# A product made in four pieces, the second half of it behind the first half's sums

## The chip, the cores and the metric

The kernel runs on one core of a Trainium2 chip. The metric is the time of one execution of the whole program on the device, in microseconds (us). Below, TensorE is PE in the profile, VectorE is DVE, ScalarE is ACT, GpSimd is POOL and SyncE is SP; a trailing "q" is the engine's sequencer.

## The reference

A graph with 12,500 nodes of 64 features and 400,000 edges, sorted by destination, goes through two graph layers with a residual and a layer norm each. The change is in the message passing of the second layer:

```
h     = x @ Wn.T + bn                                   # 12,500 x 64
w     = ssp(ssp(edge @ We1.T + be1) @ We2.T + be2)      # 400,000 x 64, ssp(z) = softplus(z) - log 2
m     = h[src] * w                                      # 400,000 x 64
agg   = segment_sum(m, dst)                             # 12,500 x 64
x     = layernorm(x + (ssp(agg @ Wc.T + bc) @ Wp.T + bp))
```

## The kernel before

The program has three long phases over the edges: two for the first graph layer (`pick_phase`, called twice) and a third, `gate_phase`, for the lines above. Each goes over 125 blocks (`NB`) of 3,200 edges, as 128 partitions with 25 edges each (the slots, `SLOTS`).

In the third phase a block n needs these things.

- **Rows.** 22 of the 25 slots of `h[src]` are gathered from `hn_table` in memory by indirect DMAs that GpSimd issues, one for each slot (L965), into the buffer `big[:, u]` with u = n mod 2. GpSimd waits on `block_used` before it begins: TensorE counts that up when it has read the second half of the sums of block n-2 (L1022). So the gather for block n+2 begins when block n's second sums are done. SyncE loads the next list of indices (L939) as soon as a gather has landed. The last three slots (`GSEL`) are picked by TensorE products with one-hot matrices (`pick`, L1002, one call for each slot) and finished on VectorE (`take`: L1148, L1159, L1162).
- **Gates.** TensorE makes the first layer's product (`first_layer`, L983) two blocks ahead, ScalarE its softplus logs (`first_logs`, L1060 to L1064), VectorE its activation (`first_activation`, L1129), TensorE the second product (`second_layer`, L990), VectorE adds the bias (`second_values`, L1136), ScalarE takes the second logs (`second_logs`, L1058 to L1064, four groups of columns, written to `lg2`), and VectorE adds the two parts (`gates`, L1143). `gates` writes over the same tile that `second_logs` writes: `gate_e` is `lg2`. So `second_logs(n+1)` must not begin before block n's gates have been read.
- **Messages.** `gate_messages` (L1190 to L1196) waits for the gather and multiplies: `big = (gate_e - log 2) * big`, all 25 slots x 64 = 1600 elements a partition in one VectorE instruction. It then counts up `gated`. TensorE waits for `gated` in `add_up(0)`, and ScalarE waits for it at the head of `second_logs(n+1)` (L1078).
- **Sums.** The slots are in two halves, 0 to 12 and 13 to 24 (`HALVES`). For each half VectorE makes a one-hot tile (`make_hot`, L1170), TensorE multiplies the messages with it (`add_up(h)`, L1018), and VectorE adds the result into `acc` (L1188).

Each engine works through its own list in a fixed order, written by hand. For block n:

```
VectorE: gate_messages(n); half(0): hot, wait for TensorE, acc; take(n+1, 0); gates(n+1);
         window loads; half(1): hot, wait for TensorE, acc; take(n+1, 1);
         first_activation(n+2); take(n+1, 2); second_values(n+2); window loads of block n+1
TensorE: pick(n+1, 0); add_up(0); pick(n+1, 1); first_layer(n+2);
         add_up(1); pick(n+1, 2); second_layer(n+2)
ScalarE: second_logs(n+1); first_logs(n+2); low_hots(n+2)
GpSimd:  gather of block n+2 once add_up(1) of block n is done
```

A "window load" is a short run of VectorE sequencer work (`windows`) that reads the bounds of a loop from memory; the engine is idle if nothing is queued before it.

Of the kernel before, what the change touches and what calls it, by code (L numbers as in the profile page):

```python
# [17 lines left out]
ALU = mybir.AluOpType  # L18
# [6 lines left out]
F = 64  # L25
H = 16
LOG2 = 0.6931471805599453
EPS = 1e-5

SLOTS = 25  # L30
# [3 lines left out]
HALVES = ((0, 13), (13, SLOTS))  # L34
GROUPS = ((0, 4), (4, 7), (7, 10), (10, 13))
NG = len(GROUPS)

WIN = 128
NW = -(-V // WIN)
# [48 lines left out]
def gnn_kernel(nc, x, xw, src, src_sel, src_gate, dst_all, edge_t, W_linT, b_lin, W1_agg, W1_root, b1, W2_parts, W2_diag, WnT, bn, We1T, be1,  # L88
               We2T, be2, WcT, bc, WpT, bp, out):
    ctx = ExitStack()  # L90
    with ctx:
# [6 lines left out]
        def sem(name):  # L98
            return ctx.enter_context(nc.semaphore(name))
# [75 lines left out]
        big = sb("big", [P, 2, SLOTS * F])  # L175
# [35 lines left out]
        waited = sem("waited")  # L211
# [655 lines left out]
        def gate_phase(tag, table, buf, hots, tiles):  # L867
# [6 lines left out]
            s1, gate_e = lg1, lg2  # L874
# [23 lines left out]
            z2_psum = sem(f"{tag}_z2_psum")  # L898
            u_made = sem(f"{tag}_u_made")
            log2_made = sem(f"{tag}_log2_made")  # L900
            gated = sem(f"{tag}_gated")
            pZ = bank[2:6]

            def turn_of(g, u):
# [17 lines left out]
            with nc.Block() as block:  # L922
# [48 lines left out]
                @block.tensor  # L971
                def _(pe):
                    pe.sem_inc(block_used, bufs)
                    pe.sem_inc(hot_used[0], 1)
                    pe.sem_inc(hot_used[1], 1)

                    def first_layer(n, turn, u):
                        pe.wait_ge(e_in[u], 16 * turn)
                        for q in range(NG):
                            cs, w = cols_of(q)  # L980

                            pe.wait_ge(u_made, NG * n + q + 1)
                            pe.matmul(pZ[q][:, 0:w], we1_2[:, :], xT_e[u][:, cs], start=True,  # L983
                                      stop=True).then_inc(z1_psum, 1)

                    def second_layer(n):
                        for q, (a, b) in enumerate(GROUPS):
                            pe.wait_ge(s1_made, NG * n + q + 1)
                            for k in range(a, b):
                                last = pe.matmul(pZ[q][:, (k - a) * P:(k - a + 1) * P], s1[:, k * P:(k + 1) * P],  # L990
                                                 we2_2[:, :], start=True, stop=True)
                            last.then_inc(z2_psum, 1)

                    def pick(n, s):
                        pe.wait_ge(low_made, GSEL * n + s + 1)
                        for c in range(2):
                            half = 2 * s + c
                            o = bank[HALF_BANK[half % 3]][:, 0:GHALF * F]
                            pe.wait_ge(pick_taken, 2 * GSEL * n + half + 1)
                            for h in range(GLOW):  # L1000
                                for part in range(2):
                                    last = pe.matmul(o, low_hot[s][:, h, :],  # L1002
                                                     hn_split[:, part, h * GHIGH + c * GHALF:h * GHIGH + (c + 1) * GHALF, :],
                                                     start=(h == 0 and part == 0), stop=(h == GLOW - 1 and part == 1))
                            last.then_inc(pick_psum, 1)

                    def add_up(h, n, u):
                        a, b = HALVES[h]
                        since, to, _ = windows(pe, n, h, False)
                        if h == 0:  # L1010
                            pe.wait_ge(gated, n + 1)
                        pe.sem_inc(waited, 1)
                        with pe.Fori(since, to) as visit:
                            pe.wait_ge(acc_added[h], visit + 1)
                            pe.wait_ge(hot_made[h], visit + 1)
                            for j in range(a, b):
                                c = (j % 2) * F
                                last = pe.matmul(sums[h][c:c + F, :], buf[u][:, j, 0:F], hots[h][:, j - a, :],  # L1018
                                                 start=(j < a + 2), stop=(j >= b - 2))
                            last.then_inc(hot_used[h], 1)  # L1020
                        if h == 1:
                            pe.drain().then_inc(block_used, 1)  # L1022

                    def body(n, g, u):
                        more = not isinstance(n, int) or n + 2 < NB
                        pick(n + 1, 0)
                        add_up(0, n, u)
                        pick(n + 1, 1)
                        if more:
                            first_layer(n + 2, turn_of(g, u) + 1, u % 2)  # L1030
                        add_up(1, n, u)
                        pick(n + 1, 2)
                        if more:
                            second_layer(n + 2)

                    first_layer(0, 1, 0)
                    second_layer(0)
                    pick(0, 0)
                    first_layer(1, 1, 1)
                    pick(0, 1)  # L1040
                    pick(0, 2)
                    second_layer(1)
                    with pe.Fori(0, turns) as g:
                        for u in range(bufs):
                            body(bufs * g + u, g, u)
                    for n in range(bufs * turns, NB - 1):
                        body(n, n // bufs, n % bufs)
                    add_up(0, NB - 1, (NB - 1) % bufs)
                    add_up(1, NB - 1, (NB - 1) % bufs)

                @block.scalar
                def _(act):
# [19 lines left out]
                    def second_logs(n):  # L1072
                        for q in range(NG):
                            cs, w = cols_of(q)

                            act.wait_ge(u_made, NG * n + q + NG + 1)
                            if q == 0 and (not isinstance(n, int) or n > 0):
                                act.wait_ge(gated, n)  # L1078
                            log_of(lg2[:, cs], u_e[:, cs], None, log2_made)

                    def low_hots(n, s, turn, u):
# [34 lines left out]
                def _(dve):  # L1116
# [59 lines left out]
                    def half(h, n, since, to, first):  # L1176
                        with dve.Fori(since, to) as visit:
                            window = nc.s_assert_within(
                                visit - since, 0, NW - 1,
                                skip_runtime_bounds_check_because="a half's dst span NW windows at most")  # L1180
                            start = nc.s_assert_within(
                                first + window * WIN, 0, V - 1,
                                skip_runtime_bounds_check_because="a visit starts at or before a dst")
                            make_hot(h, n, window, visit + 1)

                            dve.wait_ge(hot_used[h], visit + 2)
                            a_w = acc[:, bass.ds(start, WIN)]
                            dve.tensor_tensor(a_w, a_w, sums[h], ALU.add).then_inc(acc_added[h], 1)  # L1188

                    def gate_messages(n, g, u):  # L1190
                        dve.wait_ge(gathered[u], 16 * took * (g + 1))
                        dve.sem_inc(waited, 1)
                        dve.drain()
                        h = big[:, u, :]
                        dve.scalar_tensor_tensor(h, gate_e[:, 0:SLOTS * F], -LOG2, h, ALU.add,  # L1195
                                                 ALU.mult).then_inc(gated, 1)  # L1196

                    def body(n, g, u):
                        ahead = not isinstance(n, int) or n + 1 < NB
                        more = not isinstance(n, int) or n + 2 < NB  # L1200
                        since, to, first = windows(dve, n, 0, True)
                        gate_messages(n, g, u)
                        half(0, n, since, to, first)
                        if ahead:
                            take(n + 1, 0, (u + 1) % 2)
                            gates(n + 1)
                        since, to, first = windows(dve, n, 1, True)
                        half(1, n, since, to, first)
                        if ahead:
                            take(n + 1, 1, (u + 1) % 2)  # L1210
                        if more:
                            first_activation(n + 2)
                        if ahead:
                            take(n + 1, 2, (u + 1) % 2)
                        if more:
                            second_values(n + 2)
# [535 lines left out]
```

## Time and profile before

| | |
|---|---|
| median of 3 runs | 14133.36 us (14097.36 to 14136.13) |
| the profiled execution | 14125.89 us, its span 14124.2 us |
| TensorE busy | 9348.3 us, 66% |
| ScalarE busy | 6242.7 us, 44% |
| GpSimd busy | 6000.3 us, 42% |
| VectorE busy | 5042.0 us, 36% |
| mean granted TensorE clock | 0.782 of full speed |

No engine is busy for more than two thirds of the span, and the DMA engines only for a tenth or so. The first `gate_messages` of the third phase begins at 7614.7 us and the last of its 125 at 14049.6 us. In the rows below a time is the start of an instruction in us from the start of the span, then comes its length in us; x26 means that 26 such instructions ran with no gap; what stands in brackets is the idle time of the engine just before and what ended it. A TensorE row can be off in its names, since some of its records can be missing.

### The profile page before, as it was taken

How to read it: one execution, taken by the hardware profiler on the slowest of the kernel's cores; microseconds unless marked ns; L12 is line 12 of the kernel's file. 1: busy time of each engine (PE TensorE's matmuls, PEld its weight loads, DVE VectorE, ACT ScalarE, POOL GpSimd, SP SyncE). 2: the span in 40 equal slices, each digit the busy share in tenths (PEclk: the TensorE clock that was granted, in tenths of full speed). 3: DMA queues.
4: the chain of work that ended last, by engine and by line, in shares of the span. 5: the costliest groups of instructions: out<-in, count | busy, mean ns of one | idle time of the engine just before them, and what ended most of it. 6: DMA issues, size and time to landing. Idle time of an engine off the chain costs nothing. (4 is left out here: it accounts for less than half of the span.)

```text
span 14124.2 us, 173836 instructions
## 1 busy us (share of the span) xinstructions
PE 9348.3 (66%) x50412; PEld 8170.3 (58%) x50413; DVE 5042.0 (36%) x7217; ACT 6242.7 (44%) x11176; POOL 6000.3 (42%) x6363
## 2 busy tenths in 40 slices
PE   5666666666676666766676666666666666666666
PEld 5666666666666666666665554455445544555444
DVE  3333333333333333333334333333333333333334
ACT  3444444444344444444444444444444444444444
POOL 4444444444344444444433334433443334433343
PEclk8888888888788888888887777777777777777777
DMA  1111111111111111111111111111111111111111
GB/s 50 22 21 21 21 21 22 21 21 21 25 21 21 21 21 22 21 21 21 21 25 50 33 32 31 33 33 32 31 33 33 32 31 33 33 33 32 31 33 37
DMA packets 337142, 392.85 MB, mean 28 GB/s; under 512 B 163119, under 2 KB 238563, under 8 KB 336564
## 3 DMA queue, kind: packets, MB, share of 16 engines
q0 software_dynamic: 200000, 147.86, 7.2%
q1 hardware_dynamic: 136750, 244.13, 5.3%
q8 instruction: 34, 0.56, 0.0%
q14 instruction: 36, 0.29, 0.0%
q10 hardware_dynamic: 322, 0.03, 0.0%
HBM read 375.60 MB, written 15.95 MB: 28 GB/s over the span
## 5 line engine op out<-in xcount | busy, mean ns | idle before, releaser
L733 PE MATMUL banks<-split_sb,e_low_hot 128*128 128x400 f32 x22000 | 4648.8, 373 | 424.9 <-issue 357.3
L733 PEld LDWEIGHTS banks<-split_sb,e_low_hot 128*128 128x128 f32 x22000 | 4437.8, 209 | 556.9 <-issue 472.5
L965 POOL DMA_INDIRECT big<-hn_table,src_i x2750 | 2594.9, 944 | 3898.3 <-PEq L1022 3083.2
L1002 PE MATMUL banks<-hn_split,e_low_hot 128*128 128x448 f32 x10500 | 2913.9, 415 | 1996.4 <-issue 1994.8
L1002 PEld LDWEIGHTS banks<-hn_split,e_low_hot 128*128 128x128 f32 x10500 | 2232.4, 217 | 2586.9 <-issue 2428.9
L704 ACT ACTIVATE e_low_hot<-e_key_off 128x1536 fp32r<-128x1536 f16 x1000 | 1379.4, 1379 | 3719.3 <-remote 2416.1
L679 POOL DMA_INDIRECT big<-h_table,src_i x1750 | 1652.6, 944 | 1933.4 <-DVEq L846 1403.9
L679 POOL DMA_INDIRECT big<-p_table,src_i x1750 | 1652.8, 944 | 1920.5 <-DVEq L846 1394.6
L794 DVE TENSOR_REDUCE picked<-banks 128x48 f32<-128x1200 f32 x1000 | 1303.3, 1303 | 2851.9 <-remote 1834.2
L700 ACT ACTIVATE e_key_off<-e_key_in,node_off 128x384 f16<-128x384 f16 (+1 forms) x4000 | 2027.0, 577 | 127.6 <-DMA e_key_in<-sel_dram 43.7
L751 PE MATMUL banks<-hot,big 128*64 128x128 bf16 x6250 | 385.3, 259 | 1868.3 <-issue 985.6
L1058 ACT ACTIVATE e_wide<-e_wide 128x512 f32<-128x512 f32 x500 | 268.9, 538 | 2954.8 <-DVE big L1195 2922.2
L751 PEld LDWEIGHTS banks<-hot,big 128*64 128x64 bf16 x6250 | 265.4, 129 | 2024.9 <-issue 2024.6
L1136 DVE TENSOR_TENSOR e_wide<-banks,be_wide 128x512 f32<-128x512 f32 x500 | 276.2, 586 | 2555.0 <-remote 2257.6
L1089 ACT ACTIVATE e_low_hot<-spare,node_off 128x128 fp32r<-128x128 f16 x2625 | 802.5, 386 | 11.1 <-remote 11.1
L1018 PE MATMUL banks<-hot,big 128*64 128x128 f32 x6250 | 560.2, 341 | 371.9 <-DVE hot L1170 371.9
L1018 PEld LDWEIGHTS banks<-hot,big 128*64 128x64 f32 x6250 | 490.7, 175 | 500.3 <-issue 500.3
L835 DVE TENSOR_TENSOR acc<-acc,banks 128x128 f32 x500 | 144.2, 288 | 1516.9 <-PE banks L751 1073.3
L1159 DVE TENSOR_TENSOR spare<-banks,spare 128x448 f32<-128x448 f32 x750 | 445.1, 622 | 433.1 <-remote 322.0
L1060 ACT ACTIVATE e_wide<-banks,c_be 128x512 f32<-128x512 f32 x500 | 297.2, 594 | 649.4 <-PE banks L983 649.4
L1064 ACT ACTIVATE e_wide<-e_wide 128x512 f32<-128x512 f32 x1000 | 550.7, 551 | 68.0
L1062 ACT ACTIVATE e_wide<-e_wide 128x512 f32<-128x512 f32 x1000 | 550.7, 551 | 67.9
(221 smaller groups left out, 5237.0 us busy)
## 6 DMA issues: line engine op xcount, KB each, us to landing
e_wide<-in_edge_t SPq DMA_DIRECT2D x125, 832.0 KB
e_key_in<-sel_dram SPq DMA_DIRECT2D x250, 343.8 KB
big<-hn_table,src_i POOLq DMA_INDIRECT x2750
big<-p_table,src_i POOLq DMA_INDIRECT x1750
big<-h_table,src_i POOLq DMA_INDIRECT x1750
spare<-gate_dram SPq DMA_DIRECT2D x125, 96.0 KB
src_i<-in_src SPq DMA_DIRECT2D x375, 12.5 KB, 2.5
e_key_in<-sel_dram SPq DMA_DIRECT2D x250, 8.2 KB
```

The costliest lines, as they stand in the source:

```text
L679: pool.indirect_dma_start(buf[u][:, j, 0:ROW0], None, table, bass.IndirectOffsetOnAxis(ap=src_i[u][:, j:j + 1], axis=0),).then_inc(gathere ...
L700: act.activation(off[:, h, :], key_in[u][:, es], ACT.Abs, bias=node_off[:, h:h + 1])
L704: act.activation(low_hot[gr][:, :, :], off, ACT.Relu, bias=1.0, scale=-1.0).then_inc(low_made, 1)
L733: last = pe.matmul(o, low_hot[gr][:, h, e], split_sb[:, part, h * HI1:(h + 1) * HI1, :], start=(h == 0 and part == 0), stop=(h == HI2 - 1 ...
L751: last = pe.matmul(sums[h][c:c + ROW0, :], buf[u][:, j, :], hots[h][:, j - a, :], start=(j < a + 2), stop=(j >= b - 2))
L794: dve.tensor_reduce(picked[:, AT[gr]:AT[gr] + SIZE[gr], :], found, AX.X, ALU.max).then_inc(pick_taken, 1)
L965: pool.indirect_dma_start(buf[u][:, j, 0:F], None, table, bass.IndirectOffsetOnAxis(ap=src_i[u][:, j:j + 1], axis=0),).then_inc(gathered[u ...
L1002: last = pe.matmul(o, low_hot[s][:, h, :], hn_split[:, part, h * GHIGH + c * GHALF:h * GHIGH + (c + 1) * GHALF, :], start=(h == 0 and part ...
L1018: last = pe.matmul(sums[h][c:c + F, :], buf[u][:, j, 0:F], hots[h][:, j - a, :], start=(j < a + 2), stop=(j >= b - 2))
L1062: act.activation(o, o, ACT.Exp, scale=-1.0)
L1064: act.activation(o, o, ACT.Ln, bias=1.0).then_inc(made, 1)
L1089: act.activation(hot[:, h, :], key_in[u][:, s * P:(s + 1) * P], ACT.Abs, bias=node_off[:, h:h + 1])
```

## The change

The product of gates and rows is made in four instructions in place of one: slots 0 to 5 and 6 to 12 at the place where the one stood, and slots 13 to 18 and 19 to 24 after the first half's sums are in `acc` and before `take(n+1, 0)`. There are now two counters, one for each half. TensorE waits for the first in `add_up(0)` and for the second in `add_up(1)`. ScalarE, which waited for the one counter at the head of `second_logs(n+1)`, now waits for that of the second half.

```diff
+GATE_CUT = (((0, 6), (6, 13)), ((13, 19), (19, SLOTS)))
...
-            gated = sem(f"{tag}_gated")
+            gated = [sem(f"{tag}_gated{h}") for h in range(2)]
...
                     def add_up(h, n, u):
                         a, b = HALVES[h]
                         since, to, _ = windows(pe, n, h, False)
-                        if h == 0:
-                            pe.wait_ge(gated, n + 1)
+                        pe.wait_ge(gated[h], n + 1)
                         pe.sem_inc(waited, 1)
...
                             act.wait_ge(u_made, NG * n + q + NG + 1)
                             if q == 0 and (not isinstance(n, int) or n > 0):
-                                act.wait_ge(gated, n)
+                                act.wait_ge(gated[1], n)
                             log_of(lg2[:, cs], u_e[:, cs], None, log2_made)
...
-                    def gate_messages(n, g, u):
-                        dve.wait_ge(gathered[u], 16 * took * (g + 1))
-                        dve.sem_inc(waited, 1)
-                        dve.drain()
-                        h = big[:, u, :]
-                        dve.scalar_tensor_tensor(h, gate_e[:, 0:SLOTS * F], -LOG2, h, ALU.add,
-                                                 ALU.mult).then_inc(gated, 1)
+                    def gate_messages(h, n, g, u):
+                        if h == 0:
+                            dve.wait_ge(gathered[u], 16 * took * (g + 1))
+                            dve.sem_inc(waited, 1)
+                            dve.drain()
+                        for a, b in GATE_CUT[h]:
+                            m = big[:, u, a * F:b * F]
+                            last = dve.scalar_tensor_tensor(m, gate_e[:, a * F:b * F], -LOG2, m, ALU.add, ALU.mult)
+                        last.then_inc(gated[h], 1)
...
                         since, to, first = windows(dve, n, 0, True)
-                        gate_messages(n, g, u)
+                        gate_messages(0, n, g, u)
                         half(0, n, since, to, first)
+                        gate_messages(1, n, g, u)
                         if ahead:
                             take(n + 1, 0, (u + 1) % 2)
                             gates(n + 1)
```

## Rows read from the trace of the kernel before

**Rows 1.** Page: busy time of each engine, share of the span, instructions.

```profile
PE 9348.3 (66%) x50412; PEld 8170.3 (58%) x50413; DVE 5042.0 (36%) x7217; ACT 6242.7 (44%) x11176; POOL 6000.3 (42%) x6363
```

**Rows 2.** One line of the source, L1195, the product, over the whole span.

```profile
L1195 DVE SCALAR_TENSOR_TENSOR big<-e_wide,big x125: 1824/1825/1827, 7614.7 to 14049.6; 128x1600 f32<-128x1600 f32 x125
```

**Rows 3.** Timeline of all engines, block A, to its gather's landing.

```profile
10070.31 1.49 DVE L1136 TENSOR_TENSOR e_wide<-banks,be_wide 128x384 f32<-128x384 f32 x3 [5.65 <-remote]
10072.79 1.82 DVE L1195 SCALAR_TENSOR_TENSOR big<-e_wide,big 128x1600 f32<-128x1600 f32 x1 [0.99 <-issue]
10074.53 1.94 DVE L1170 SCALAR_TENSOR_TENSOR hot<-dst_f,win_base,banks 128x1664 f32<-128x1664 f32 x1
10074.71 0.63 ACT L1058 ACTIVATE e_wide<-e_wide 128x512 f32<-128x512 f32 x1 [23.07 <-DVE big L1195]
...
10076.62 3.07 PE L1018 MATMUL banks<-hot,big 128*64 128x128 f32 x26 [1.71 <-DVE hot L1170]
...
10079.91 0.29 DVE L1188 TENSOR_TENSOR acc<-acc,banks 128x128 f32 x1 [3.44 <-PE banks L1018]
...
10081.00 0.53 ACT L1064 ACTIVATE e_wide<-e_wide 128x384 f32<-128x384 f32 x1
...
10082.82 2.09 DVE L1143 SCALAR_TENSOR_TENSOR e_wide<-e_wide 128x512 f32<-128x512 f32 x4
10084.82 1.80 DVE L1170 SCALAR_TENSOR_TENSOR hot<-dst_f,win_base,banks 128x1536 f32<-128x1536 f32 x1
...
10085.40 2.96 PE L983 MATMUL banks<-e_wide,we 128*128 128x512 f32 x8
...
10088.29 1.53 PE L1018 MATMUL banks<-hot,big 128*64 128x128 f32 x24
...
10090.69 0.94 POOL L965 DMA_INDIRECT big<-hn_table,src_i  x1 [24.40 <-PEq L1022]
...
10119.51 0.33 SPq L939 DMA_DIRECT2D src_i<-in_src  x1
```

**Rows 4.** Timeline of all engines, block B, the next one.

```profile
10124.81 1.82 DVE L1195 SCALAR_TENSOR_TENSOR big<-e_wide,big 128x1600 f32<-128x1600 f32 x1 [1.50 <-issue]
...
10128.64 1.71 PE L1018 MATMUL banks<-hot,big 128*64 128x128 f32 x26 [1.87 <-DVE hot L1170]
...
10130.58 0.29 DVE L1188 TENSOR_TENSOR acc<-acc,banks 128x128 f32 x1 [2.08 <-PE banks L1018]
...
10133.03 0.53 ACT L1064 ACTIVATE e_wide<-e_wide 128x384 f32<-128x384 f32 x1
...
10136.29 1.81 DVE L1170 SCALAR_TENSOR_TENSOR hot<-dst_f,win_base,banks 128x1536 f32<-128x1536 f32 x1 [0.70 <-issue]
...
10138.95 1.53 PE L1018 MATMUL banks<-hot,big 128*64 128x128 f32 x24
...
10141.40 0.94 POOL L965 DMA_INDIRECT big<-hn_table,src_i  x1 [23.57 <-PEq L1022]
...
10175.07 1.82 DVE L1195 SCALAR_TENSOR_TENSOR big<-e_wide,big 128x1600 f32<-128x1600 f32 x1 [1.76 <-issue]
```

**Rows 5.** Timeline of all engines, block C, one with late second sums.

```profile
10905.98 1.82 DVE L1195 SCALAR_TENSOR_TENSOR big<-e_wide,big 128x1600 f32<-128x1600 f32 x1 [0.98 <-issue]
...
10913.25 0.29 DVE L1188 TENSOR_TENSOR acc<-acc,banks 128x128 f32 x1 [3.59 <-PE banks L1018]
...
10922.94 1.53 PE L1018 MATMUL banks<-hot,big 128*64 128x128 f32 x24
...
10925.34 0.94 POOL L965 DMA_INDIRECT big<-hn_table,src_i  x1 [25.82 <-PEq L1022]
...
10959.50 1.82 DVE L1195 SCALAR_TENSOR_TENSOR big<-e_wide,big 128x1600 f32<-128x1600 f32 x1 [1.90 <-issue]
```

**Rows 6.** Windows: us, busy us (instructions) of five engines, PEclk, DMA, GB/s.

```profile
10076.00:10079.00 3.00, 2.38 (x23) 2.41 (x25) 0.47 (x1) 2.73 (x7) 0.00 (x0) 0.50 0.00 0
10088.00:10090.00 2.00, 1.82 (x26) 1.29 (x24) 0.00 (x0) 1.86 (x4) 0.00 (x0) 1.00 0.35 57
```

## The prediction

> **What bounds the kernel now.** I read the page first. No engine is busy for more than two thirds of the span, and VectorE, which does the changed work, for 36% [rows 1]. So the kernel is held by an order of waits, and a saved microsecond counts only where it stands on that order. The view of the one source line gives the frame: 125 products of 1.82 us each, the first at 7614.7 us and the last at 14049.6 us [rows 2]. That is 6434.9 us over 124 steps, 51.9 us a block, and the change touches nothing outside this stretch.
>
> Then I read the timeline of three blocks and wrote every event as a distance from the start of the block's product. In block A [rows 3]: first one-hot tile 1.74, first sums on TensorE 3.83, first add into `acc` 7.12, `gates` 10.03, second one-hot tile 12.03 to 13.83, `first_layer` 12.61 to 15.57, second sums 15.50, first gather instruction 17.90, gather landed 46.72 (SyncE's next index load), next block's product 52.02. The reader is to see three things.
>
> First, from 17.90 on only the gather counts. It takes 28.8 us to land, and the product comes 5.3 us after the landing (10119.51 and 10124.81), just behind the last groups of `second_values` (the first row of block A, released 2.48 us before its product). From the gather's start to the next product it is 34.1 us in A, 33.7 in B and 34.2 in C, while the gather's start itself is at 17.9, 16.6 and 19.4 [rows 3 to 5]. The block lengths follow: 52.0, 50.3 and 53.5 us. A block is the gather's start plus about 34 us. I don't know why `second_values`, whose input comes from TensorE alone, waits that long; the release is shown as "remote". But the sum holds in three blocks whose gather starts 2.8 us apart, and both readings (the release waits for the gather, or for TensorE's own work behind the second sums) move with the second sums.
>
> Second, the second sums wait for TensorE, not for VectorE. In A the second one-hot tile is done at 13.83 and TensorE comes at 15.50, straight from `first_layer`. That is a slack of 1.7 us; it is 0.7 us less the usual handover in B, where the tile ends at 13.29 and TensorE comes at 14.14 [rows 4].
>
> Third, ScalarE stood idle for 23.07 us and begins `second_logs` 1.92 after the product's start, on the product's own signal. Its four groups take until 8.74, that is 6.82 us, and lie under the first one-hot tile, the first sums and `take` [rows 3].
>
> **The change part by part.** *Shorter first product.* In block A 1600 elements cost 1.74 us from start to next start, and four instructions with 1664 elements together 2.09 us to their end [rows 3]; the one long one needs 1.82 to its end, so the last end adds 0.08. The two equations (1600 c + k = 1.74 and 1664 c + 4 k = 2.01) give c = 1.045 ns an element and k = 0.07 us an instruction. Slots 0 to 5 are 384 elements, 0.47 us; slots 6 to 12 are 448, 0.54 us. The first one-hot tile starts at 1.00 in place of 1.74: 0.74 us saved. TensorE waited 1.71 us for that tile in A and 1.87 in B, so it takes all of it. If instructions did not overlap at all I would add 0.08 for each, and save 0.66; that is the lower bound.
>
> The Trainium skill, VectorE: DVE Perf Modes, The DRAIN you can't avoid, says that a next operation does not start until the pipeline has emptied. The trace differs: the one-hot tile starts 1.74 us after a product that lasts 1.82 [rows 3]. By the page the saving would be the 0.66 us just bounded.
>
> *Second product.* It starts where `take` started, 0.29 us after the first add, and its two pieces of 384 elements need 0.47 and 0.55: the second signal comes 1.31 us after the start of the add. In A that is 7.12 - 0.74 + 1.31 = 7.69.
>
> *The moved wait of ScalarE.* This is the term that decides. `second_logs(n+1)` may not write the gates' tile before the second product has read it, so it begins 0.10 us after that signal (1.92 against 1.82 before), at 7.79 and no longer at 1.92. After 6.82 us the last group is ready, at 14.61. What lies behind the wait on ScalarE, `first_logs` and `low_hots`, starts a little later too: its first input is ready about when `first_layer` starts, 12.61 - 0.74, and it now waits until 14.61. Its results are needed by `second_layer` and the next `pick`, behind the second sums, which move further than that; I price it at nothing. SyncE's two waits on these have tens of microseconds in hand.
>
> *VectorE behind it.* `take(n+1, 0)` is cover of some 2.7 us only; then `gates` waits group by group for ScalarE. Behind the last of those waits stand the window loads and the second one-hot tile. Block B shows this chain when ScalarE is the last: its last log ends at 10133.56 and the second tile starts at 10136.29, 2.73 us later, with VectorE idle for 0.70 of it [rows 4]. So in A the tile starts at 14.61 + 2.73 = 17.34, ends 1.81 later, and TensorE, by the 0.15 us from tile end to first sums in A, starts the second sums at 19.30. Before it was 15.50: 3.80 us later. `pick(n+1, 2)`, `second_layer` and the drain that lets the gather go are queued behind them.
>
> *By block.* New start = old first add + 12.18 us. A: 19.30, B: 17.95, C: 19.45, against 15.50, 14.14 and 16.96 [rows 3 to 5]. The second sums are 3.8, 3.8 and 2.5 us later, on average 3.4. C is less since TensorE was late there anyway.
>
> *The clock.* TensorE now has nothing to do from 15.57 - 0.74 = 14.83 to 19.30, 4.5 us in each block. In A the clock was at 0.50 (1.2 GHz) in the first sums, behind a wait of 1.71 us, and at 1.00 in the second ones [rows 6]; 26 matmuls took 3.07 us there, while in B they took 1.71 after a wait of 1.87 us. So after a wait the clock may be at either level. The second sums, 24 matmuls, would take 3.07 x 24 / 26 = 2.83 us at the lower one in place of 1.53: 1.3 us more, at most. The first sums could gain as much in blocks where their shorter wait keeps the clock up. I take 0.4 net, three blocks in ten, between the ends 0 and 1.3.
>
> *Sum.* 3.4 + 0.4 = 3.8 us a block for the 123 blocks that start a gather: 467 us. The profiled execution took 14125.9 us (span 14124.2), which gives 14593; it is 7 us under the median of the runs, inside their spread of 39 us. I predict 14590 us, 3.2% more.
>
> **The rivals.** *The low clock in every block.* For it: an idle stretch of 4.5 us, longer than the 1.71 before the slow first sums of A. Against it: B, fast after 1.87. Price: (3.4 + 1.3) x 123 = 578 us, 14704 us. The Trainium skill, TensorE: Matmul & The Clock Gate, What's actually happening, has the default clock throttled and activity releasing it; by that rule the second sums behind the new wait would be the slow ones, and rows 6 agree for the first sums of A.
>
> *Partly given back.* The time from the gather's start to the product shrinks when the start is late, say because part of what VectorE and ScalarE do behind it was late for its own reasons. A third to two thirds of 3.4 us, 14270 to 14410 us. Against it: 34.2 us in C, the block with the latest start.
>
> *Nothing is passed on.* The next product is set by something that does not move with the second sums. Then the 3.4 us vanish in the 34, and the time is 14126 us. The three block lengths speak against it.
>
> *Faster.* The first sums come 0.74 us sooner, and with them `pick`, `first_layer`, the second sums and the gather: 123 x 0.74 = 91 us, 14035 us. One thing decides: the second tile must be ready when TensorE arrives, at 15.50 - 0.74 = 14.76 in A. It needs 12.18 us from the old first add and may take 7.64. ScalarE's 6.82 us would have to be 2.3, or `second_logs` start before the second product, which its wait forbids.
>
> **How the numbers follow.** The forecast has 0.70, the low clock 0.12, partly given back 0.10, nothing passed on 0.04, faster 0.04. The forecast's own range comes from 2.9 to 4.7 us a block: all blocks like C with the clock term give 2.5 + 0.4, and the clock rival is the upper end: 14480 to 14704. With a little of the partial case below and a margin above, 14440 to 14730 us holds it 8 times in 10. A measurement of this kernel tells about 0.3%, 42 us, from no change: faster 0.04, same 0.04, slower 0.92.
>
> **What would show it.** In the new profile: two pairs of products in a block, near 1.0 us each pair; the first one-hot tile 1.00 us after the first piece; ScalarE's first log of `second_logs` 7.8 us after it (6.4 in blocks like B) and its idle time before grown; VectorE idle between the four `gates`, released by ScalarE; the second tile at 17.3, TensorE's second sums near 19.3 with the tile named as the releaser; the gather's start near 21.7, and 34 us from there to the next product. The clock row of the second sums tells the clock term. The prediction is wrong if those 34 us shrink, or if the second sums still follow `first_layer` without a wait.

## The result and the profile after

| | before | after |
|---|---|---|
| median of 4 runs each, side by side | 14115.88 us (14097.36 to 14136.13) | 14649.35 us (14623.76 to 14671.31) |
| ratio, 95% interval | | 1.0376 (1.0364 to 1.0388) |
| the profiled execution | 14125.89 us | 14671.31 us, its span 14669.6 us |
| mean granted TensorE clock | 0.782 | 0.772 |

The change makes the kernel 3.8% slower. The forecast was 14590 us, in the range 14440 to 14730 us; the measured time is 59 us above the forecast and inside the range. The two profiled executions differ by 545 us, 4.43 us for each of the 123 blocks, and the medians by 533 us, 4.34 us a block, where the forecast had 3.8.

In the comparisons below the kernel before takes about 14,120 us in some and about 8,320 us in others, once each way on the same chip, so every ratio is taken only against the runs of the kernel before that stood beside it, and each experiment says which of the two it met.

The page after, busy time of each engine; it answers to [rows 1]:

```profile
PE 9567.3 (65%) x50412; PEld 8315.3 (57%) x50413; DVE 5104.3 (35%) x7592; ACT 6240.6 (43%) x11176; POOL 6000.2 (41%) x6363
```

VectorE has 375 instructions more, three a block, and 62.3 us more work, 0.5 us a block. ScalarE and GpSimd have the same work as before. The 545 us are waits, and the slower clock in which TensorE's 219 us more are spent. The waits of the third phase after, from the view of waits (engine, line, what released it: us in total, times, longest):

```profile
ACT e_wide L1058 <- DVE big L1197: 3903.3, 124, 33.4
POOL big L966 <- PEq L1022: 3616.1, 123, 47.9
...
PE banks L1018 <- DVE hot L1170: 998.4, 248, 13.1
...
DVE e_wide L1143 <- ACT e_wide L1064: 326.1, 372, 1.0
DVE hot L1170 <- issue: 264.4, 124, 2.2
```

Before, the same view of the same phase had ScalarE at 2922.2 us behind the product, GpSimd at 3083.2 us behind TensorE, TensorE at 360.3 us in 125 waits behind the one-hot tile, no wait of `gates` for ScalarE at all, and 9.8 us idle before the second one-hot tile. The reader is to see the new chain in these five rows: ScalarE starts later (+981 us; in exchange its 642.7 us of waiting for TensorE's `first_layer`, 123 times, is gone), `gates` now waits for it (three times a block, since the first of the four logs is ready), the second tile stands behind the window loads (2.1 us a block; the row says "issue", and that it is the loads is read from the order of the code), TensorE waits for that tile as well as for the first (248 waits, not 125), and GpSimd waits 533 us more, 4.3 us a block.

The timeline after, one block, answers to [rows 3]; a time is the start, then come the length, and in brackets the idle time before and its releaser:

```profile
10104.17 1.09 DVE L1197 SCALAR_TENSOR_TENSOR big<-e_wide,big 128x384 f32<-128x384 f32 x2 [2.29 <-issue]
10105.18 1.94 DVE L1170 SCALAR_TENSOR_TENSOR hot<-dst_f,win_base,banks 128x1664 f32<-128x1664 f32 x1
...
10107.27 3.22 PE L1018 MATMUL banks<-hot,big 128*64 128x128 f32 x26 [10.34 <-DVE hot L1170]
...
10110.71 0.29 DVE L1188 TENSOR_TENSOR acc<-acc,banks 128x128 f32 x1 [3.59 <-PE banks L1018]
10110.92 1.02 DVE L1197 SCALAR_TENSOR_TENSOR big<-e_wide,big 128x384 f32<-128x384 f32 x2
...
10112.03 0.63 ACT L1058 ACTIVATE e_wide<-e_wide 128x512 f32<-128x512 f32 x1 [32.23 <-DVE big L1197]
...
10117.36 2.96 PE L984 MATMUL banks<-e_wide,we 128*128 128x512 f32 x8
...
10118.33 0.52 ACT L1064 ACTIVATE e_wide<-e_wide 128x384 f32<-128x384 f32 x1
...
10118.89 0.56 DVE L1143 SCALAR_TENSOR_TENSOR e_wide<-e_wide 128x384 f32<-128x384 f32 x1 [1.03 <-ACT e_wide L1064]
...
10121.59 1.81 DVE L1170 SCALAR_TENSOR_TENSOR hot<-dst_f,win_base,banks 128x1536 f32<-128x1536 f32 x1 [2.14 <-issue]
...
10123.55 2.83 PE L1018 MATMUL banks<-hot,big 128*64 128x128 f32 x24 [3.23 <-DVE hot L1170]
...
10127.29 0.94 POOL L966 DMA_INDIRECT big<-hn_table,src_i  x1 [29.80 <-PEq L1022]
```

Counted from the product's start: first tile 1.01, second product 6.75, ScalarE's first log 7.86 (before 1.92), its last log over at 14.68, the second tile 17.42 (before 12.03), second sums 19.38 (before 15.50), gather 23.12 (before 17.90). The next product came at 10160.84, 33.55 us after the gather's start. And the second sums take 2.83 us where they took 1.53 [rows 3]. The windows after show the clock in which they ran (us, busy us with counts of PE, PEld, DVE, ACT, POOL, then the granted clock, DMA share, GB/s); they are the first sums, `first_layer`, the two halves of the gap behind it, and the second sums:

```profile
10107.30:10110.50 3.20, 3.20 (x27) 2.87 (x27) 0.00 (x0) 0.00 (x0) 0.00 (x0) 0.50 0.00 0
10117.40:10120.30 2.90, 2.90 (x9) 1.29 (x7) 1.01 (x2) 2.63 (x6) 0.00 (x0) 1.00 0.00 0
10120.40:10122.00 1.60, 0.00 (x0) 0.00 (x0) 0.41 (x1) 1.47 (x4) 0.00 (x0) 1.00 0.41 71
10122.00:10123.50 1.50, 0.00 (x0) 0.00 (x0) 1.40 (x1) 1.43 (x3) 0.00 (x0) 0.91 0.91 346
10123.60:10126.40 2.80, 2.78 (x24) 2.38 (x24) 0.00 (x0) 2.66 (x7) 0.00 (x0) 0.50 0.14 59
```

`first_layer` still ran at 1.00; the clock fell while TensorE did nothing, and the second sums found it at 0.50.

One block can mislead, so the same distances were taken as means over the 121 blocks in the middle of the phase. "Gather" is the first gather instruction, and the last column is the granted clock over the first / second sums:

| us from the product's start | ScalarE's first log | second sums | add into `acc` | gather | gather to next product | block | clock |
|---|---|---|---|---|---|---|---|
| before | 1.92 | 15.80 | 17.57 | 18.23 | 33.9 | 52.14 | 0.59 / 1.00 |
| after | 7.69 | 19.21 | 21.97 | 22.63 | 33.8 | 56.46 | 0.55 / 0.58 |

Second sums 3.41 us later, then 0.99 us more from them to the add, and 0.07 us less from the gather to the next product: 4.33 us a block.

### The profile page after: what moved, and what is told of

The parts are those of the page before. It is cut to its first block and busy times, and to the rows that moved or that the text cites. A ratio compares the mean times of both kernels' runs of the same rounds, so it can differ in the third digit from the quotient of the medians.

```text
span 14669.6 us, 174336 instructions
## 1 busy us (share of the span) xinstructions
PE 9567.3 (65%) x50412; PEld 8315.3 (57%) x50413; DVE 5104.3 (35%) x7592; ACT 6240.6 (43%) x11176; POOL 6000.2 (41%) x6363
## 5 line engine op out<-in xcount | busy, mean ns | idle before, releaser
L1003 PE MATMUL banks<-hn_split,e_low_hot 128*128 128x448 f32 x10500 | 2987.1, 422 | 1682.8 <-issue 1679.9
L1018 PE MATMUL banks<-hot,big 128*64 128x128 f32 x6250 | 697.7, 399 | 1003.1 <-DVE hot L1170 1003.0
L1018 PEld LDWEIGHTS banks<-hot,big 128*64 128x64 f32 x6250 | 608.1, 209 | 1166.0 <-issue 1166.0
L1170 DVE SCALAR_TENSOR_TENSOR hot<-dst_f,win_base,banks 128x1664 f32<-128x1664 f32 x250 | 469.2, 1877 | 265.6 <-issue 265.6
```

The lines of the kernel that those rows point to most:

```text
L1003: last = pe.matmul(o, low_hot[s][:, h, :], hn_split[:, part, h * GHIGH + c * GHALF:h * GHIGH + (c + 1) * GHALF, :], start=(h == 0 and part ...
```

## The experiments

Lines in the rows of an experiment are shifted by one to three where its edit adds lines.

**1. All four pieces ahead of the first sums** (met 8,320 us). Pieces without the move:

```diff
                         gate_messages(0, n, g, u)
+                        gate_messages(1, n, g, u)
                         half(0, n, since, to, first)
-                        gate_messages(1, n, g, u)
```

> All four pieces stand ahead of the first sums; the two counters stay. My theory (the moved wait of ScalarE costs the time): ScalarE's second logs may begin 1.9 to 2.0 us after the first piece again, the second one-hot tile is ready before TensorE, and only three more instructions at 0.07 us are left, 0.2 us a block, 25 us: ratio to the kernel before about 1.002, at most 1.004. Rival (the pieces themselves, or the second wait of TensorE, cost the time): the ratio stays near 1.038.

Measured: 8319.01 us against 8322.64 us, ratio 0.9995 (0.9986 to 1.0005). Four instructions and two counters show no cost in the time when they all stand ahead. That is less than "they cost nothing": in this condition GpSimd's issue of the gather fills the block (see the last section), and the second sums, which in the mean start 14.42 us after the product's start here and 14.18 us after it in experiment 4, can be 0.24 us later unseen. The forecast 0.2 us for three more instructions is thus neither shown nor refuted. ScalarE begins 0.18 us after the first tile's start, as before the change. The changed kernel itself loses 7.4% in this condition (experiment 12), so the loss comes with the place of the second pair.

**2. The late wait alone** (met 8,320 us). The kernel before, whole product in one instruction, but ScalarE is let go behind the first half's sums:

```diff
+            gates_free = sem(f"{tag}_gates_free")
...
-                                act.wait_ge(gated, n)
+                                act.wait_ge(gates_free, n)
...
                         gate_messages(n, g, u)
                         half(0, n, since, to, first)
+                        dve.drain().then_inc(gates_free, 1)
```

> The kernel before with its one long product where it was, and only ScalarE's wait moved: it now waits for a drain that VectorE executes behind the first half's sums. My theory: second logs begin 0.4 to 0.5 us after the start of the first add into acc, at 7.5 us in the block, and end 6.8 later; the second tile starts 2.7 us after that, at 17.1; TensorE's second sums start near 19, 3.2 us later than before, and run at a lower clock in most blocks for 1 us more. That is 4.2 to 4.4 us a block, ratio 1.037 (1.030 to 1.042), though the product is not cut at all. Rival (it is the cut or the second product's place on VectorE): ratio within 1.003.

Measured: 8822.62 us against 8322.64 us, ratio 1.0602 (1.0585 to 1.0618), 500 us more or 4.07 us a block. The ratio lies above the expected range, which was reckoned for 14,120 us; in us a block it is a little under the expected 4.2 to 4.4. Its timeline, one block:

```profile
6009.15 1.71 PE L1019 MATMUL banks<-hot,big 128*64 128x128 f32 x26 [0.52 <-DVE hot L1171]
...
6011.52 0.63 ACT L1059 ACTIVATE e_wide<-e_wide 128x512 f32<-128x512 f32 x1 [8.24 <-DVEq L1205]
...
6021.08 1.81 DVE L1171 SCALAR_TENSOR_TENSOR hot<-dst_f,win_base,banks 128x1536 f32<-128x1536 f32 x1 [2.15 <-issue]
...
6023.04 2.83 PE L1019 MATMUL banks<-hot,big 128*64 128x128 f32 x24 [3.41 <-DVE hot L1171]
...
6026.73 0.94 POOL L966 DMA_INDIRECT big<-hn_table,src_i  x1 [4.47 <-PEq L1023]
```

Nothing is left of the change here but ScalarE's wait, and the whole picture of the changed kernel is back: the tile that is 2.15 us late behind the window loads, TensorE's wait of 3.41 us, second sums of 2.83 us, and GpSimd's wait. Shown, in this condition: the moved wait alone makes this chain.

**3. The changed kernel with the gates in a tile of their own** (met 8,320 us). The order of the four pieces is kept, and ScalarE needs no wait, since it no longer writes what the product reads. Some tiles that only the set-up uses were moved to memory that is freed after it, to make room.

```diff
-            s1, gate_e = lg1, lg2
+            s1 = lg1
+            gate_e = tiles.enter_context(nc.sbuf_tensor(f"{tag}_gate", [P, XE], F32))
...
-                            if q == 0 and (not isinstance(n, int) or n > 0):
-                                act.wait_ge(gated[1], n)
```

> The changed kernel, but gates writes a tile of its own, so second logs need not wait for any product. My theory: ScalarE starts the second logs before the block's first product; the second tile is ready at 14.0 us in a block like A and TensorE arrives from first_layer at 14.8, so the 0.74 us of the shorter first product reach the second sums and the gather: 0.74 x 123 = 91 us less than the kernel before, ratio 0.994 (0.991 to 0.997). Rival (the saving is lost elsewhere, in the gather or on VectorE): ratio 1.000. Rival (the second product's place on VectorE costs the time): ratio near 1.038.

Measured: 8270.32 us against 8322.64 us, ratio 0.9936 (0.9923 to 0.995). The loss is gone and a gain of 52 us stands in its place. The ratio is the expected one, but by luck: the expectation had 91 us, from first sums 0.74 us earlier, for a kernel of 14,126 us. Here the block goes from 28.23 us (experiment 4) to 27.85, and the last section puts those 0.38 us down to the length of GpSimd's gather instructions.

**4. The same tile and no wait in the kernel before** (met 8,320 us). The set-up tiles are moved as in experiment 3.

```diff
-            s1, gate_e = lg1, lg2
+            s1 = lg1
+            gate_e = tiles.enter_context(nc.sbuf_tensor(f"{tag}_gate", [P, XE], F32))
...
-                            if q == 0 and (not isinstance(n, int) or n > 0):
-                                act.wait_ge(gated, n)
```

> The control for the one before: the kernel before with the gates' own tile and without ScalarE's wait, the product uncut. My theory: the wait was not on the order that sets the end there, so the ratio is 1.000 (0.998 to 1.002), and the gain of the tile with the cut product is the cut's own. Rival (ScalarE's earlier start alone brings time): ratio under 0.997.

Measured: 8320.49 us against 8322.64 us, ratio 0.9998 (0.9989 to 1.0007). ScalarE's early wait was free, so the 52 us of experiment 3 belong to the split of the product and not to the tile. This control was not run at 14,120 us.

**5 and 6. The changed kernel and the kernel before, again** (met 14,120 us). Nothing edited; they give the traces that the next two are read against.

> The changed kernel itself, again. Where the kernel before takes 8322 us, its third phase goes at 28.2 us a block (measured with the own tile, which made no difference) and the gather is issued without a pause. My theory: the second sums still start 12.18 us behind the old first add, 3.8 us later than before, whatever the chip's state, and the wait of ScalarE makes it; moving that wait alone cost 500 us there, 4.07 us a block. The change also shortens the first product by 0.74 us on the same chain: 3.3 us a block, 410 us, ratio 1.049 (1.040 to 1.060). Rival (the loss belonged to the slow releases of the first chip alone): ratio under 1.01.

> The kernel before, for its rows on this chip. If it is the chip of the last runs: 8322 us, a block of 28.2 us, GpSimd's instructions for the gather 0.3 us apart with no wait for TensorE, one of them lengthened by 0.6 us in each block while VectorE makes the long product. If it is the first chip: 14116 us and a block of 51.9 us.

Measured: 14642.73 us against 14121.19 us, ratio 1.0376 (1.0358 to 1.0393), block 56.37 us; and 14105.5 us in one run, block 52.27 us. Both repeat the result.

**7. One gather instruction less** (met 14,120 us). On top of experiment 3, 21 slots are gathered in place of 22, and the two waits for the gather count one less; the slot left out keeps old rows, and this work is missing from its time.

```diff
-                        for j in range(took):
+                        for j in range(took - 1):
```

> The changed kernel with the gates' own tile, but the gather leaves out one of its 22 slots (that slot keeps old data). My theory for the chip of the last runs: with the wait gone, GpSimd's issue of the gather sets the block of 27.84 us, 22 instructions 1.25 us apart; one less takes off 1.25 us until TensorE's own order becomes the bound: 0.6 to 1.25 us a block, ratio 0.978 to 0.988. Rival (TensorE already sets it): ratio 0.9936 as with 22.

Measured: 13690.25 us against 14121.19 us, ratio 0.9696 (0.968 to 0.9712). The expected 0.978 to 0.988 was for the other condition. Against experiment 9, the same kernel with 22 slots in the same condition, its block is 48.71 us and not 50.60, and the gather's start to the next first tile 33.52 us and not 34.99. One gather instruction and the gap behind it are 1.25 us, and they account for most of these 1.47 us. Another 0.35 us is the first sums at a higher clock, 0.90 in place of 0.79. That higher clock was not explained. The stretch of "about 34 us" behind the gather's start follows the gather's length.

**8. TensorE kept busy in the new gap** (met 14,120 us). The changed kernel, with 14 matmuls of no use between `first_layer` and `add_up(1)` (the trace shows two records for each such matmul, x28 below):

```diff
                             first_layer(n + 2, turn_of(g, u) + 1, u % 2)
+                            pe.wait_ge(pick_taken, 2 * GSEL * (n + 1) + 5)
+                            for _ in range(14):
+                                pe.matmul(bank[1][:, 0:WIN], we2_2[:, :], ident[:, :], start=True, stop=True)
                         add_up(1, n, u)
```

> The changed kernel, with 14 matmuls of 128 columns without use (3.3 us) on TensorE between first_layer and the wait for the second half's product. They fill the idle stretch and delay nothing, if TensorE is idle there for 4 us. My theory: the clock of the second sums stays at 1.00 and these take 1.8 us to the add in place of up to 2.8: 0.5 to 1.0 us a block less than the changed kernel beside it, 60 to 120 us. Rival (the clock has no part in the loss): the same time as the changed kernel.

Measured: 14530.26 us against 14121.19 us, ratio 1.0289 (1.0272 to 1.0306), and 112 us less than the changed kernel beside it, 0.91 us a block. Its timeline:

```profile
10120.40 3.29 PE L1033 MATMUL banks<-ident,we 128*128 128x128 f32 x28
...
10124.69 1.53 PE L1018 MATMUL banks<-hot,big 128*64 128x128 f32 x24 [1.00 <-DVE hot L1173]
10126.44 0.29 DVE L1191 TENSOR_TENSOR acc<-acc,banks 128x128 f32 x1 [1.90 <-PE banks L1018]
...
10127.08 0.94 POOL L966 DMA_INDIRECT big<-hn_table,src_i  x1 [28.18 <-PEq L1022]
```

The second sums still wait 1.00 us for the tile, but take 1.53 us, at a granted clock of 1.00 in the mean of all blocks. From their start to the add it is 1.76 us, as before the change, and no longer 2.76. The clock term is thus shown by itself: it is 0.91 us a block. The expected 60 to 120 us held.

**9 and 10. Own tile and changed kernel side by side** (met 14,120 us). The kernels of experiment 3 and of the change.

> The changed kernel with the gates' own tile once more, for the condition in which the kernel before takes 14100 us (a block of 52.1 us, set by the gather's start plus 34). My theory for that condition: the 0.74 us of the shorter first product reach the gather, 91 us, and since the first sums ran at a higher clock in the run with 21 rows (0.90 against 0.59) up to 0.95 us a block more: ratio 0.985 to 0.994. Rival (there the second product's place costs something even without the wait): ratio over 1.000. Where the kernel before takes 8322 us it is a repetition, 0.994.

> The changed kernel once more, for the condition in which the kernel before takes 8322 us (a block of 28.2 us, set by the gather's issue). My theory: the second sums start 3.8 us later, with some at a lower clock, and a block is no longer set by the gather: late wait alone cost 4.07 us a block there, less 0.74 for the shorter product gives 3.3: ratio 1.049 (1.040 to 1.058). Rival (the loss belongs to the other condition alone): ratio under 1.01. Where the kernel before takes 14100 us it is a repetition, 1.038.

Measured: own tile 13948.5 us against 14132.15 us, ratio 0.9869 (0.9853 to 0.9886); changed 14681.26 us, ratio 1.0389 (1.0372 to 1.0407). They differ in ScalarE's wait and the tile that makes it needless (with the set-up tiles moved for it), and by 733 us or 6.0 us a block. The own-tile kernel, one block:

```profile
10148.38 3.22 PE L1020 MATMUL banks<-hot,big 128*64 128x128 f32 x26 [1.85 <-DVE hot L1170]
10151.83 0.29 DVE L1188 TENSOR_TENSOR acc<-acc,banks 128x128 f32 x1 [3.59 <-PE banks L1020]
10152.03 1.02 DVE L1197 SCALAR_TENSOR_TENSOR big<-e_gate,big 128x384 f32<-128x384 f32 x2
...
10157.72 1.81 DVE L1170 SCALAR_TENSOR_TENSOR hot<-dst_f,win_base,banks 128x1536 f32<-128x1536 f32 x1
```

The second tile starts 5.69 us after the second product here and 10.67 us after it in the changed kernel, and there is no idle time before it. Its mean block is 50.60 us, 1.54 less than before: 0.74 from the shorter first product, and 0.60 from the first sums, whose mean granted clock is 0.79 and no longer 0.59. TensorE's idle time just before them is 1.72 us in the mean here and 2.91 us before the change. Why their clock is higher I did not test. The remaining 0.2 us lie between the first add and the second sums (8.52 us, before 8.80), less 0.08 us more behind the gather's start.

**11 and 12. Late wait and changed kernel side by side** (met 8,320 us). The kernels of experiment 2 and of the change. They were meant for the other condition, so the late wait alone was not measured at 14,120 us.

> ScalarE's wait moved alone, once more, for the condition in which the kernel before takes 14100 us. The long product stays whole and first. My theory: the second sums start 0.1 us behind a second tile that is ready 19.7 us after the product's start (old first add 7.1, drain and signal 0.5, second logs 6.8, window loads 2.7, tile 1.8 and 0.8 of slack in the estimate), 3.9 us later than 15.8, and run at a lower clock for 1.0 more: 4.5 to 4.9 us a block, 550 to 600 us, ratio 1.041 (1.035 to 1.046), a little more than the change costs, for it lacks the shorter first product. Rival (the loss there comes from the cut or from the second product's place): ratio under 1.01. Where the kernel before takes 8322 us it is a repetition, 1.060.

> The changed kernel beside it, for the difference of the two on one chip: my theory is that it takes 0.5 to 1.0 us a block less than the kernel with the late wait alone, the 0.74 us of the shorter first product, so a ratio to the kernel before of 1.038 where that takes 14100 us, and of 1.049 (1.040 to 1.058) where it takes 8322. Rival (the cut gives nothing back): the same time as with the late wait alone.

Measured: late wait 8825.29 us against 8320.44 us, ratio 1.061 (1.0592 to 1.0627); changed 8934.99 us, ratio 1.0738 (1.072 to 1.0756). The late wait repeats experiment 2. The changed kernel misses what I expected (1.040 to 1.058, and 0.5 to 1.0 us a block below the late wait for its shorter first product); it is 110 us above the late wait, 0.9 us a block. First the late wait, then the changed kernel, one block each:

```profile
6005.48 1.93 DVE L1171 SCALAR_TENSOR_TENSOR hot<-dst_f,win_base,banks 128x1664 f32<-128x1664 f32 x1
...
6007.56 1.71 PE L1019 MATMUL banks<-hot,big 128*64 128x128 f32 x26 [0.53 <-DVE hot L1171]
...
6009.93 0.63 ACT L1059 ACTIVATE e_wide<-e_wide 128x512 f32<-128x512 f32 x1 [8.25 <-DVEq L1205]
...
6021.46 2.83 PE L1019 MATMUL banks<-hot,big 128*64 128x128 f32 x24 [3.41 <-DVE hot L1171]
```

```profile
6008.98 1.94 DVE L1170 SCALAR_TENSOR_TENSOR hot<-dst_f,win_base,banks 128x1664 f32<-128x1664 f32 x1
...
6011.07 1.71 PE L1018 MATMUL banks<-hot,big 128*64 128x128 f32 x26 [0.30 <-DVE hot L1170]
...
6014.33 0.63 ACT L1058 ACTIVATE e_wide<-e_wide 128x512 f32<-128x512 f32 x1 [8.92 <-DVE big L1197]
...
6025.83 2.83 PE L1018 MATMUL banks<-hot,big 128*64 128x128 f32 x24 [4.38 <-DVE hot L1170]
```

From the first tile ScalarE starts at 4.45 in the one and at 5.35 in the other, and the second sums at 15.98 and 16.85. The 0.9 us is the second product, which in the changed kernel stands in ScalarE's way. In the means the second sums are 0.98 us later and 0.3 us slower, and only 0.39 of the 0.74 us from the shorter first product comes back. Part of it was nothing to win here: TensorE waited 0.53 us for the first tile with the long product. That TensorE's `pick` of the next block holds the rest is what the short wait (0.30) suggests; I did not test it.

## Why the prediction was right, and what was mis-sized

**The first product.** Forecast: the first tile 1.00 us after it. Measured: 1.01 (10104.17 and 10105.18). The slope and offset from [rows 3] held, and so did the reading that VectorE's instructions overlap by 0.08 us (0.74 us saved and not 0.66). The Trainium skill, VectorE: DVE Perf Modes, The DRAIN you can't avoid, does not contradict this, as the prediction had it: behind the sentence that the prediction took, the same paragraph says that a next op that is not held starts earlier, and the trace agrees, since the tile starts 1.01 us after two pieces that last 1.09 us together.

**The moved wait.** Forecast in block A: ScalarE at 7.79, its last group over at 14.61, the second tile at 17.34, TensorE at 19.30. The block shown has 7.86, 14.68, 17.42 and 19.38. In the mean the second sums came 3.41 us later, and the forecast had 3.4 from three blocks. From the first add to them it is 12.84 us in the mean; the forecast's 12.18 + 0.74 is 12.92. Experiment 2 makes this chain with the wait alone, and experiments 3 and 9 take it away by freeing ScalarE from the wait and keeping all else. At 14,120 us the direct proof is the pair 9 and 10; neither the late wait alone nor the own tile in the kernel before was measured there, so the tile's own part in these 6.0 us is known only from experiment 4, where it was nothing.

**Work behind ScalarE's wait priced at nothing.** Held: from the gather's start to the next product the mean is 33.8 us, where it was 33.9 and "about 34" was forecast. Experiment 7 adds what the prediction left open: this stretch shrinks with the gather, by 1.47 us for 1.25 us of gather. "Nothing is passed on" and "partly given back" fall with it.

**The clock: the term that was mis-sized.** The prediction took 0.4 us net, "three blocks in ten", between 0 and 1.3. Measured: the second sums run at a mean granted clock of 0.58 and not 1.00, and take 0.99 us more to the add. The first sums gain nothing in return: their clock is 0.55 in place of 0.59, and they take 0.10 us more to the add, which is inside the 3.41. Experiment 8, which fills the gap, gives 0.91 us. The sum with the measured term is 3.41 + 0.99 - 0.07 = 4.33 us a block, and 4.33 x 123 = 533 of the 545 us; of the other 12 us, 7.8 us lie ahead of the phase, since its first product begins at 7622.4 and not 7614.7 us. The rival with the low clock in every block had 4.7 us, 14704 us, and the truth lies between it and the forecast, nearer to the rival in this term. What misled was block B: it stayed fast after a wait of 1.87 us [rows 4], and I let one fast block after a wait weigh as much as one slow one, although the new gap was longer than either. That gap was mis-sized too, without effect on the time: 4.5 us in the forecast, 3.82 us in the mean and 3.23 in the block shown, where `first_layer` came 13.19 us after the product and not 11.87. The Trainium skill, TensorE: Matmul & The Clock Gate, What's actually happening, has activity release a clock that is throttled by default, and the runs agree: 0.58 behind the empty gap, 1.00 behind the filled one.

**Faster.** The rival needed ScalarE freed from the wait. Experiments 3 and 9 are that case: 0.9936 and 0.9869, the first of them by another way than the rival's. At 14,120 us the kernel gains 184 us, twice the 91 us that the rival had: the rival's 0.74 us a block are there, and 0.60 us come from the higher clock of the first sums, which it did not have.

## What to carry to other kernels

When an operation is split so that its first part releases a consumer sooner, list who waits for its last part: here the gain was 0.74 us and the price 3.4 us plus the clock, because another engine writes over the tile that the last part still reads. A buffer of its own for that tile turned the same split from 3.8% slower into 1.3% faster. And price a new gap on TensorE at the low clock for the work right behind it, until a trace of such a gap says otherwise.

## What the runs showed of the hardware

**Two conditions of one program.** The kernel before took 8322.64 us in one comparison and 14121.19 us in a later one on the same chip. At 8,320 us the page of experiment 4, the kernel before with its own tile, reads:

```profile
PE 7891.1 (95%) x50412; PEld 7216.5 (87%) x50413; DVE 5017.2 (60%) x7217; ACT 6232.4 (75%) x11176; POOL 6117.3 (74%) x6363
```

The counts are those of [rows 1], TensorE is nearly always busy, and its mean granted clock is 0.984. At 14,120 us TensorE's `pick` matmuls come one by one while a gather is in flight, with 1.57 us of idle time before most of those in the block shown that the trace calls "issue", and `second_values` is let go by "remote" 15.12 us after VectorE's work before it:

```profile
10113.35 0.53 PE L1002 MATMUL banks<-hn_split,e_low_hot 128*128 128x448 f32 x1 [1.56 <-issue]
...
10115.46 0.53 PE L1002 MATMUL banks<-hn_split,e_low_hot 128*128 128x448 f32 x1 [1.57 <-issue]
...
10116.18 0.69 DVE L1136 TENSOR_TENSOR e_wide<-banks,be_wide 128x512 f32<-128x512 f32 x1 [15.12 <-remote]
```

The three other groups of `second_values` start at 10121.82, 2.31 us behind the gather's landing (10119.51 [rows 3]), when TensorE's matmuls follow each other again. I read from this that the gather in flight slows TensorE's work behind the second sums, and that a block there is the gather's start plus 34 us for that reason; experiment 7 fits it, but no run separates the two. What brings the one or the other condition about stays open; no experiment here chose it. The change loses in both, by 1.038 and 1.074.

**A gather instruction can get longer beside VectorE's product or `gates`.** At 8,320 us GpSimd issues without a pause, 22 x 1.25 = 27.5 us of a block of 28.2; with the longer ones it is a mean of 1.287 us from start to start, 28.3 us, in experiment 4, and 1.269 us, 27.9, in experiment 3. Experiment 4 in that condition:

```profile
6009.38 0.94 POOL L967 DMA_INDIRECT big<-hn_table,src_i  x1 [0.30 <-issue]
6009.47 1.82 DVE L1195 SCALAR_TENSOR_TENSOR big<-e_gate,big 128x1600 f32<-128x1600 f32 x1 [2.46 <-DMA big<-hn_table,src_i]
6010.63 1.48 POOL L967 DMA_INDIRECT big<-hn_table,src_i  x1 [0.31 <-issue]
```

The instruction that falls on the end of the product and the start of the tile behind it takes 1.48 us and not 0.94; the one before it, which lies beside the product alone, takes 0.94. In experiment 4, 198 of the 2750 take over 1.1 us: 124 of them where the product meets the first tile, and 68 where `gates` meets the second. In experiment 3 it is 135, of which 119 where `gates` meets the second tile and 11 beside a piece of the product. So the pieces take away the first kind, and it is not a matter of the product's length alone: the same happens beside `gates`, whose pieces are 384 and 512 elements. The mean of the 2750 is 982 ns in experiment 4, 965 ns with the pieces in experiment 3, and 944 ns at 14,120 us, where no gather is being issued when the product runs. (982 - 965) ns x 2750 = 47 us is about the 50 us by which experiment 3 is faster than experiment 4. That this is the cause is argued from these numbers; what the two engines share I did not test.

**Window loads cost what stands in front of them.** Idle before the second tile was 9.8 us in the whole phase before and 264.4 us after, 2.1 us a block. The same loads stand in both programs; before, they were covered, since VectorE had work queued ahead of them.
